# A decoder block on one core: the cross-attention query split in its PSUM bank and copied straight into the stack, with half of the next self-attention query ahead of the norm's transposes

## The reference, cut to what matters

```python
ct_q = x @ Wd_q_w + Wd_q_b
query = heads(ct_q @ Wu_q_w + Wu_q_b) + heads(_rope(ct_q @ Wq_r_w + Wq_r_b, cos, sin))
ct_kv = x @ Wd_kv_w + Wd_kv_b
key = heads(ct_kv @ Wu_k_w + Wu_k_b) + heads(_rope(x @ Wk_r_w + Wk_r_b, cos, sin))
value = heads(ct_kv @ Wu_v_w + Wu_v_b)
...
x = _layernorm(x + self_attention)
q = (x @ W0.T + b0).reshape(B, Sq, H, dk).transpose(0, 2, 1, 3)      # cross query
k = (ctx @ W1.T + b1) ... ; v = (ctx @ W2.T + b2) ...
scores = where(mask == 0, NEG, q @ k.T / sqrt(dk)); p = softmax(scores)
x = _layernorm(x + (p @ v) @ W3.T + b3)
x = _layernorm(x + ffn(x))
```

## Time and profile before

| what | value |
|---|---|
| three runs | 1837.96, 1840.87, 1842.05 us; median 1840.87 |
| profiled execution | 1838.62 us; span 1836.5 us, mean granted clock 0.926 |
| PE busy | 1602.8 us (87%) |
| DVE busy | 1241.5 us (68%) |
| ACT busy | 888.1 us (48%) |
| POOL busy | 431.8 us (24%) |

### The profile page before, as it was taken

One profiled execution on the slowest core, in us unless ns is written; L12 is line 12 of the kernel. 1 busy time (PEld: TensorE's weight loads), 2 busy tenths in 40 slices (PEclk: granted clock), 3 DMA queues, 4 the chain that ended last, 5 costly groups with the idle time before them and its releaser, 6 DMA issues. The chain is left out here.

```text
span 1836.5 us, 26832 instructions
## 1 busy us (share of the span) xinstructions
PE 1602.8 (87%) x9790; PEld 789.6 (43%) x9790; DVE 1241.5 (68%) x2136; ACT 888.1 (48%) x1582; POOL 431.8 (24%) x543
## 2 busy tenths in 40 slices
PE   7499999797999997979999979899997687999993
PEld 3023324445223244452332444523323436888872
DVE  5588854875788758757888587578877644664443
ACT  2067784351677742526777425267774251111111
POOL 4300003402000035011000350110002301566663
PEclk9589999897999998978999989789999797999996
DMA  5800001814000018231000182310000413455594
GB/s 183 183 8 1 2 1 55 207 45 114 20 1 2 1 50 207 51 93 41 2 1 2 44 208 56 93 41 1 1 2 12 111 48 104 85 106 115 113 266 115
DMA packets 108255, 128.21 MB, mean 70 GB/s; under 512 B 17244, under 2 KB 81756, under 8 KB 108124
## 3 DMA queue, kind: packets, MB, share of 16 engines
q1 hardware_dynamic: 95836, 109.71, 21.7%
q0 software_dynamic: 12288, 16.79, 5.5%
HBM read 84.49 MB, written 40.79 MB: 68 GB/s over the span
## 5 line engine op out<-in xcount | busy, mean ns | idle before, releaser
L965 ACT ACTIVATE pT<-banks 128x512 f32<-128x512 f32 x1184 | 645.1, 595 | 280.1 <-PE banks L1639 167.8
L1172 DVE TENSOR_REDUCE nmf<-banks 128x1 f32<-128x1024 f32 x512 | 604.8, 1220 | 138.9 <-PE banks L1581 137.7
L1639 PE MATMUL banks<-qst,kst 99*128 99x512 bf16 x1024 | 350.3, 389 | 16.5 <-DMA qst<-nmT 7.1
L1581 PE MATMUL banks<-kst,qst 96*128 96x512 bf16 x1024 | 327.9, 405 | 33.0 <-DMA kst<-k_parts 23.0
L1673 PE MATMUL banks<-pT,V 128*32 128x512 f32 x2048 | 274.6, 608 | 17.3 <-ACT oT L953 12.2
L1639 PEld LDWEIGHTS banks<-qst,kst 99*128 99x128 bf16 x1024 | 96.0, 97 | 310.8 <-ACT pT L965 186.7
L784 POOL CAST nmp<-nmf 128x16 bf16<-128x16 f32 x64 | 12.8, 200 | 834.3 <-issue 760.9
L1581 PEld LDWEIGHTS banks<-kst,qst 96*128 96x128 bf16 x1024 | 98.6, 101 | 149.2 <-DVE nmf L1172 37.1
L1167 DVE TENSOR_REDUCE nmf<-banks 128x4 f32<-128x616 f32 x128 | 99.8, 798 | 62.7 <-PE banks L1575 55.1
L1041 ACT ACTIVATE kst<-banks 128x512 f32<-128x512 f32 x64 | 38.1, 597 | 203.3 <-PE banks L1903 177.3
L973 ACT ACTIVATE nmT<-banks 6x1024 bf16<-6x1024 bf16 x64 | 64.8, 1013 | 135.0 <-PE banks L1623 111.0
(11 more groups left out here) (201 smaller groups left out, 2218.0 us busy)
## 6 DMA issues: line engine op xcount, KB each, us to landing
qst<-q_parts SPq DMA_DIRECT2D x48, 256.0 KB, 6.4
kst<-k_parts SPq DMA_DIRECT2D x48, 256.0 KB, 4.5
qst<-in_w SPq DMA_DIRECT2D x16, 512.0 KB
qxs<-in_w SPq DMA_DIRECT2D x16, 512.0 KB
q_parts<-kst SPq DMA_DIRECT2D x48, 128.0 KB, 2.4
qxs<-qx_parts SPq DMA_DIRECT2D x24, 256.0 KB, 4.9
qst<-qx_parts SPq DMA_DIRECT2D x24, 256.0 KB
kst<-in_xT SPq DMA_DIRECT2D x4, 1024.0 KB, 5.0
```

What stands on the lines that cost most here:

```text
L965: act.activation(pT[:, n % RING_P, :], PS[:, banks[what, n], :], ACT.Exp, scale=scale).then_inc(s_ex, 1)
L1172: dve.tensor_reduce(nmf[:, m % 2, j, t:t + 1], scores.rearrange("p a n -> p (a n)"), AX.X, ALU.max, negate=True).then_inc(s_smu, 1)
L1581: ins = pe.matmul(pair[:, half, :], qst[0:KQ, h, t * P:(t + 1) * P], kst[0:KQ, h, half * N:(half + 1) * N], start=True, stop=True)
L1639: ins = pe.matmul(ps, kst[0:KM, head, kc * P:(kc + 1) * P], qst[0:KM, head, cols], start=True, stop=True)
```

## The change

1. **The cross query's parts.** Its rows are reordered on the host (dimension by dimension instead of head by head), so that partition d*8+h of a part belongs to row d, head h of the stack. ACT writes the top part from the bank (`cross_part`), PE subtracts it in the same bank by a matmul with minus the identity (`subtract`, `minusb`), ACT writes the middle part, PE subtracts, ACT writes the low part. The parts lie in SBUF (`xparts_at`, in `oT`), and SP copies each straight into the stack: 24 copies of 128 KB in place of 12 stores of 128 KB and 12 loads of 256 KB a transition. POOL has no part in it any more.
2. **The order on PE.** The first half of the next batch's query (items q 0 to 3) stands ahead of the turned norm; the third and fourth cross items stand behind the values; their subtractions stand behind smax 1 and smax 3.
3. **Values.** ACT copies them out of the banks in place of DVE; POOL adds their bias later (`bias_values`), between the splits of groups 3 and 4.
4. **POOL.** The add of z and bias (`after_layernorm`) stands between the splits of groups 1 and 2 of cross-attention, not ahead of the pieces; mask and residual of the next batch stand between the first groups of its self-attention.
5. **SP.** The next batch's query load for heads 0 to 7 waits for the stores of all eight pieces and stands between the copies of groups 0 and 1's maxima; each third of the keys moves one group later.

```diff
-EACH = Plan(OUT_SELF + LATENTS + INTO_CROSS + OPERANDS, OUT_CROSS + CONTEXT + ROUTING)
+EACH = Plan(OUT_SELF + LATENTS + HALF_Q + TURNED + HALF_X + HALF_Q + KEYS + VALUES + HALF_X,
+            OUT_CROSS + CONTEXT + ROUTING)
...
@@ SP, rest_of_batch
+                def load_cross(i):
+                    mc, half = divmod(i, 2)
+                    rows = qxs[:, :, :] if mc == 0 else heads_of(qst, 1)
+                    wait_apart(sp, s_eva, at.taken("A", at.nth("qx", i) + 1))
+                    for t, term in enumerate(TERMS):
+                        sp.dma_start(rows[t:KQ:len(TERMS), :, half * N:(half + 1) * N], xparts_at[:, i, term[0], :]
+                                     ).then_inc(s_qx[i], 16)
                 if more:
-                    store_cross(range(9, 13))
+                    store_piece((b + 1, 0))
+                    store_piece((b + 1, 1))
                     load_cross(0)
-                    store_front(b + 1, range(4))
                     load_cross(1)
-                    stored(b + 1, 3)
-                    load_stack(heads_of(qst, 0), q_parts, 0, 0, s_ql[0])
-                    store_front(b + 1, range(4, 8))
+                    for i in range(2, 6):
+                        store_piece((b + 1, i))
+                    load_cross(2)
+                    load_cross(3)
+                    store_piece((b + 1, 6))
+                    store_piece((b + 1, 7))
                 load_minus_max(b, NG, cross_rows(0))
                 for g in range(1, NG):
-                    if more and g < NG - 1:
-                        load_keys(b + 1, range(g - 1, g))
+                    if more and g == 1:
+                        stored((b + 1, 7))
+                        load_stack(heads_of(qst, 0), q_parts, 0, 0, s_ql[0])
+                    elif more:
+                        load_keys(b + 1, range(g - 2, g - 1))
                     load_minus_max(b, NG + g, cross_rows(g))
...
@@ POOL, batch
-                pool.wait_ge(s_ln, b * 2 * T + T)
-                pool.tensor_tensor(xb[:, :, :], z[:, :, :], brow[:, 3:4, :].to_broadcast([P, T, D]),
-                                   ALU.add).then_inc(s_xb, 1)
-                split(b, 9, 13)
-                if more:
-                    split(b + 1, 0, 8)
+                split([(b + 1, i) for i in range(8)] if more else [])
...
+                split_max(b, SM_SELF, NG, cross, range(1, 2))
+                after_layernorm(b)
+                split_max(b, SM_SELF, NG, cross, range(2, 4))
                 if more:
+                    bias_values(b + 1)
+                split_max(b, SM_SELF, NG, cross, range(4, NG))
...
@@ ACT
+            def cross_part(at, b, i, part):
+                idx = at.nth("qx", i)
+                if part == 0:
+                    taken_before(at, idx)
...
+                else:
+                    act.wait_ge(s_xs[i], 2 * b + part)
+                ins = act.activation(xparts_at[:, i, part, :], PS[:, at.bank(idx), :], ACT.Identity,
+                                     bias=bcol[:, 12 + i // 2:13 + i // 2])
+                ins.then_inc(s_xt[i] if part < 2 else s_eva, 1)
...
@@ PE
+            def subtract(at, b, i, part):
+                pe.wait_ge(s_xt[i], 2 * b + part + 1)
+                pe.matmul(PS[:, at.bank(at.nth("qx", i)), :], minusb[:, :], xparts_at[:, i, part, :],
+                          start=False, stop=True, skip_group_check=True).then_inc(s_xs[i], 1)
...
                     if what == "smax":
                         maximum(b, n0, n, cross)
+                        if order is ORDER_AHEAD and n in (1, 3):
+                            for i in (2, 3):
+                                subtract(at, b, i, n // 2)
...
                 else:
+                    rank_ties(EARLY * E, EARLY * TURNS + 1)
+                    subtracted((0, 1), 0)
+                    cross_query(2)
+                    cross_query(3)
+                    subtracted((0, 1), 1)
+                    subtracted((2, 3), 0)
+                    subtracted((2, 3), 1)
+                    rank_chosen(EARLY * E, EARLY * TURNS + 2)
```

More of the change, by code:

```diff
@@ L901, in part1 @@
                 else:
-                    biased(at, b, i)
+                    biased(at, piece)
                     act.wait_ge(s_eva, at.taken("A", at.piece(i) + 1))
@@ L923, in biased @@
-                ins.then_inc(s_eva, 1)
-            def part2(b, i):
-                p, cols = i % 2, C * SK if i == 8 else N
-                _, middle, _ = parts_of(i)
-                act.wait_ge(s_p2, b * PIECES + i + 1 + START)
-                act.activation(middle, rest[:, p, 0:cols], ACT.Copy).then_inc(s_p3, 1)
+                for c in range(C):
+                    ins = act.activation(full[:, n % 2, c * SK:(c + 1) * SK], ps[:, c * SK:(c + 1) * SK],
+                                         ACT.Identity, bias=bcol[:, 10 + c:11 + c])
@@ new lines, in part2, with values @@
+            def part2(piece):
+                n, cols = NUMBER[piece], C * SK if piece[1] == 8 else N
+                _, middle, _ = parts_of(piece)
+                act.wait_ge(s_p2, n + 1 + START)
+                act.activation(middle, rest[:, n % 2, 0:cols], ACT.Copy).then_inc(s_p3, 1)
+            def values(at):
+                for k in range(4):
+                    idx = at.nth("v", k)
+                    taken_before(at, idx)
+                    act.activation(V[:, 2 * k:2 * k + 2, :, 0:HD],
+                                   PS[:, at.bank(idx), :].rearrange("p (t h d) -> p t h d", t=2, d=HD),
+                                   ACT.Copy).then_inc(s_eva, 1)
@@ L952, in empty @@
                         act.wait_ge(s_hv, b * 2 * NG + g0 + k + 1 - NG)
+                    if n0 and k == 2:
+                        for i in range(4):
+                            act.wait_ge(s_qx[i], 96 * b + 96)
                     act.activation(oT[:, k, :], PS[:, AV_BANK, :], ACT.Copy).then_inc(s_ave, 1)
@@ L975, in attention, with parts @@
                 empty(units - 1)
[L977 to L982 removed]
+            def parts(at, pieces):
+                for step in range(len(pieces) + 1):
+                    if step < len(pieces):
+                        part1(at, pieces[step])
+                    if step > 0:
+                        part2(pieces[step - 1])
             def heads_in_place(at, name):
@@ L1018, in rest_of_batch @@
                 if more:
-                    attention(b + 1, 0, 0, ST_SELF, ORDER_NEXT, BANKS_NEXT, SCALE_SELF, 9)
+                    attention(b + 1, 0, 0, ST_SELF, ORDER_NEXT, BANKS_NEXT, SCALE_SELF, NUMBER[b + 1, 8] + 1)
             act.wait_ge(s_wa, 48)
             latents(Place(FIRST))
-            parts(Place(FIRST), 0, 0, 9)
+            parts(Place(FIRST), [(0, i) for i in range(8)])
+            act.wait_ge(s_ms, 1)
+            values(Place(FIRST))
+            parts(Place(FIRST), [(0, 8)])
             attention(0, 0, 0, ST_SELF, ORDER_SELF, BANKS_SELF, SCALE_SELF, 9)
@@ L1559, in maximum @@
                         pe.wait_ge(s_mask, b + 1 + START)
-                        pe.wait_ge(s_qx[g * G // 8], b * 96 + 96)
+                        for half in range(HALVES):
+                            pe.wait_ge(s_qx[g * G // 8 * HALVES + half], b * 96 + 96)
                         pe.wait_ge(s_kx, b * 192 + 192)
@@ L1586, in cross_q, with attention @@
                 return qxs[:, h, :] if h < H // 2 else qst[:, h, :]
-            def attention(b, n0, u0, g0, order, cross):
+            def attention(b, n0, u0, g0, order, cross, at=None):
                 per = (ST_CROSS if cross else ST_SELF) // NG
@@ L1618, in attention @@
                         m = g0 + n
+                        if cross and n == 0:
+                            taken_upto(at, at.nth("qx", 3) + 1)
                         pe.wait_ge(s_nm, b * 2 * NG + m + 1)
@@ L1669, in attention @@
                             pe.wait_ge(s_pe2, 1 + START)
+                        if n == 0 and not cross:
+                            pe.wait_ge(s_vb, b + 1)
                         av = PS[:, AV_BANK, :]
```

282 lines of the change are left out of this document (155 added, 127 removed).

## The result

The changed kernel takes 1853.88 us (median of six runs, 1850.87 to 1860.74), the kernel before 1841.82 beside it. The ratio is 1.0072, 95% interval 1.0053 to 1.0092: some 13 us slower. The profiled execution spans 1853.7 us, 17.2 more than the one of before.

A forecast was written before the change was run, and what follows sets the result against it. The prediction took SP's queue, when it gets group 1's rows of maxima through, to bound the kernel. From 1838.6: -2.4 (queue), +4.5 (clock), +1.5 (last transition), +0.6 (first batch) gave 1842.8, so 1843 us; range 1829 to 1857.

The forecast's parts named there:

- SP's queue: Each transition: group 1's rows, behind copies, stores and query loads, arrive at 364.2 against 365.03; 0.8 us gained, -2.4 in all.
- the clock: PE stands 5 us or more before group 1's rows, then runs at half clock: 1.5 us a transition, +4.5 in all.
- the first batch: Piece 7's last subtraction waits on POOL behind piece 8's and ACT's copies of values: +0.6 us, bounds 0 and 3.
- the last transition: DVE loses collisions with POOL, but PE's second ranking comes later: +1.5 us, bounds -3 and +4.
- Half of the query ahead: Front of each transition: DVE's ropes begin earlier, so cross-attention starts at 336.3, 7.7 us earlier.
- The Trainium skill's rate: About 358 GB/s from HBM for the six query loads, 4.4 us in place of 7.2, giving 1834; not adopted.
- Cross items 2 and 3, POOL: PE's eight subtractions cost under 2 us a transition, inside waits; POOL's add and values' bias cost nothing.
- the copies are slow: Rival: SBUF-to-SBUF copies take twice the time, rows come 6.0 us later, 1863; chance 0.22 for 1850 and up.
- The start's gain arrives: Rival: group 1's rows land before about 357, so the earlier cross-attention start is kept, 1822; chance 0.07.

The follow-up runs named there:

- rows0_before_stores: loads_between_rows with group 0's rows of maxima also ahead of the six stores of the key's last two pieces: 1826.22 us, ratio 0.9911.
- all_mended: rows0_before_stores with the last transition and first batch reordered, POOL's adds and PE's second subtractions of items 2 and 3 later: 1817.38 us, ratio 0.9874.
- between_and_late: all_mended, but POOL's two adds where the change put them and group 0's rows behind the stores again: 1823.26 us, ratio 0.9907.
- before_rows_first: The kernel before the change, with each group's rows of maxima ahead of the key loads and store wait before them: 1836.13 us, ratio 0.9984.
- rows1_before_loads: The changed kernel with group 1's rows ahead of the store wait and six query loads, later rows ahead of their key loads: 1824.9 us, ratio 0.9911.
- loads_between_rows: rows1_before_loads with the six query loads issued two at a time behind the rows of groups 1, 2 and 3: 1824.53 us, ratio 0.9906.
- stores_by_act: all_mended with the six stores of the key's pieces 6 and 7 issued by ACT instead of SP: 1821.44 us, ratio 0.9898.

## Why the prediction was right in kind and wrong about the size

The limit was the one forecast, SP's queue in front of group 1's rows, and 1853.9 lies inside the range of 1829 to 1857. But 1843 was 11 too low, and "slower" was given little more than "same". 3 us of the 11 are the start of the sum, a single execution of 1838.6 where the kernel before has a median of 1841.8. The rest is the change itself: 4.2 us were forecast, 12 to 13 were measured, and the traces show 13.7. Of these 9.5 us too few, 7.3 are SP's queue, 1.3 the clock, 0.7 the first batch and 0.2 the last transition. The forecast of "slower" stood on the clock's term (without it the sum is 0.3 us below the start), since the queue's had the wrong sign, and the range reached as far as 1857 for slow copies, which did not happen: that the time lies inside it is partly luck. By its own steps:

- **Half of the query ahead.** Right: 7.9 us earlier, forecast 7.7.
- **SP's queue.** The failed step. Forecast was 0.8 us gained at the fourth copy in each transition, 2.4 in all; 2.2, 1.0 and 1.7 were lost, 4.9 in all, so the term was off by 7.3 us. The copies cost what I said (0.64 us to issue, eighteen copies and stores 11.5 us from 343.69), and from the first query load to the fourth copy it took 9.8 us (358.78 to 368.55), forecast 9.9. Two terms in batch 0 were short. The third item's last part was ready 1.4 us later than forecast (343.7, against 341.0 plus the shift of 1.3), since ACT waits for POOL's subtractions of piece 7 between its passes. And "the last store, issued at 351.9, lands 2.4 us later" took the page's median for one transfer: SP waited from the last store's issue at 354.6 until 358.8, 4.2 us. The earlier trace rows held the better number, a last key store issued at about 354.0 and landed at 359.95. A median over 48 issues says little of the last of a burst, and that one ends a wait. The two terms make up the 3 us of batch 0; batches 1 and 2, where the fourth copy is 1.8 and 2.5 us later than forecast, were not taken apart in this way.
- **The clock.** Right in kind: PE at 0.50 in the windows behind the wait. From the fourth to the fifth copy it is 4.6 us before, and 6.0, 6.5 and 7.2 after, so 1.4, 1.9 and 2.6; 5.8 in all, forecast 4.5. The half clock also lasted longer in batches 1 and 2: batch 0 has 0.77 in the window from 372 to 374, 3.5 to 5.5 us behind its fourth copy, and they have 0.51 and 0.50 at the same distance (743 to 745 and 1117 to 1119).
- **The Trainium skill's rate.** The six loads took the time of the rows' 217 GB/s (222 GB/s in the window from 362 to 368, at a DMA share of 1.06). The Trainium skill (DMA: Bandwidth & Descriptors, Specifications) lists 358 GB/s as the limit of one core from HBM. These loads stay far below it, and the stores of the earlier trace rows, at 379 GB/s in a window of 2 us, go above it. So it was no price for this shape, as weighed.
- **Cross items 2 and 3, POOL.** The eight subtractions were put at under 2 us. PE's line for them shows eight of 0.38 us or more (0.61 at half clock) in batch 0, some 3 us. The changed kernel hides the stall for the last of them, since its third copy waits 5.23 us for rows anyway. Taken away, that stall was worth 2.6 us at the first copy (42.3 us behind the latents in rows0_before_stores, 39.7 in all_mended and 39.8 in between_and_late). POOL's adds ended none of the waits for rows here, as said.
- **The last transition.** +1.5 forecast: 0.8 to the first scores, and 0.9 between its first and its last copy to nmT, 1.7 together. These are near the spread: in the other five traces with the same last transition the last copy comes 80.6 to 81.6 us behind DVE's last normalising (81.3 in the changed kernel), with the old one 79.6 and 80.3. Its parts were off: PE picked 24.8 us behind DVE's last normalising, where it was 22.9 before and the forecast had 23.9, since the eight projections of items 0 and 1 took 6.40 us, and DVE waited 5.06 and 6.52.
- **The first batch.** +0.6 at the first scores (70.48, against 69.92), +1.3 at the end of its self-attention, and that stands already at its second copy to nmT (117.03, against 115.65). That copy comes at 116.5 to 118.6 in the other traces with the changed first batch, and at 115.2 in before_rows_first, so the loss is real but not known to better than a microsecond. It was not traced to an instruction.

Of the rivals, "the copies are slow" gave 1851 for halfway (halfway between 1842.8 and 1863 is 1853), near the result by another road: the copies are not slow. Twelve of them and six stores were issued in 11.5 us as forecast, and 128 KB land in 2.4 us by the page's median. "The start's gain arrives" needed a chain 7 us shorter; rows1_before_loads gave that by order alone (fourth copy at 54.0 us in batch 0, against 61.0), and its 1822 stands against 1824.9 measured.

## What to carry to other kernels

Where an in-order queue feeds several consumers, write down for each transfer who waits for it and when. A short transfer with an early consumer (here 6 rows of maxima) behind a wait for stores and bulk loads with a late one cost more (29 us) than the changed kernel gains with its queue mended (16 us). Mend the queue before judging a change upstream of it: the same edits were worth +13 us or -16 us against the kernel before, depending only on whether the rows of maxima stood behind or ahead of the loads. Take the time of a transfer that ends a wait from the wait, not from a median. And compare kernels at the end of the stage that they share: over three batches the fifth copies of rows1_before_loads and loads_between_rows were 7 us apart, the eighth copies and the times were not.

## What was not expected of the hardware

- A store of 128 KB to DRAM landed in 2.3 to 3.9 us behind copies from SBUF to SBUF, and in 5.3 to 9.2 behind 256 KB loads in the kernel before: the landing time goes with what is still under way in front of it (these cases alone show it, no run varied it by itself). Line views of the key's stores in the changed kernel, from 345 to 361 us, and in the kernel before (there over twelve stores):

```profile
L559 SPq DMA_DIRECT2D k_parts<-pT x6: 598/603/615, 351.4 to 354.6; - x6
...
DMA to landing us min/median/max: 2.3/2.4/3.9
```

```profile
L545 SPq DMA_DIRECT2D k_parts<-pT x6: 597/598/612, 346.4 to 349.6; - x6
L545 SPq DMA_DIRECT2D k_parts<-kst x6: 598/605/1143, 350.2 to 354.0; - x6
...
DMA to landing us min/median/max: 5.3/7.4/9.2
```

- A transfer that ACT issues takes ACT 0.60 to 0.65 us (five in 3.27), and its next instruction waits behind it (3.32 us in front of the copy to nmT).
- Half clock comes behind short pauses of PE too: behind 2.06, 2.26 and 2.70 us in the three batches of stores_by_act and 2.40 in batch 2 of all_mended (0.50 to 0.52 in the windows behind them). In batches 0 and 1 of all_mended, where PE stood 1.01 and 1.45 us, it kept the full clock. Where PE sets the pace behind the pause, as here, the fifth copy to nmT is up to 3 us later.
- From the second to the eighth copy to nmT of a self-attention, a stretch that takes the same 144.4 us in both kernels, it is 145.8 to 146.1 in 10 of the 44 batches of eleven traces, with no pattern by kernel (the kernel before has two of them, the changed kernel none). Some microseconds between two profiled executions come from such steps, so single spans are no measure of a change of this size.
